# A reordered expert loop with a lag of three, and a narrow selecting matmul in the rotary attention

## The chip, the cores and the metric

The kernel runs on one core of one Trainium2 chip. The metric is device time in microseconds (us), from the start to the end of one execution. Besides TensorE (PE), VectorE (DVE), ScalarE (ACT) and GpSimd (POOL) the core has SyncE (SP), which here only issues DMAs.

## The reference, cut to what matters

Four layers, each an attention-like part and a feed-forward-like part with a layer norm before and after and a residual sum. The activations are 4096 tokens of 128 numbers. Two of the eight parts are touched.

```python
def _L2_ffn_ref(x, gate_w, ln_w, ln_b, fc1s, b1s, fc2s, b2s):   # expert choice: 8 experts, each takes its 512 best tokens
    scores = jax.nn.softmax(xf @ gate_w.T, axis=-1)
    vals, idx = jax.lax.top_k(scores.T, k)
    y = xf[flat_idx].reshape(k, n, d)
    y = (y - mu) * jax.lax.rsqrt(var + LN_EPS) * ln_w + ln_b
    h = jax.nn.gelu(jnp.einsum('knd,nfd->knf', y, fc1s) + b1s, approximate=True)
    out = (jnp.einsum('knf,ndf->knd', h, fc2s) + b2s) * kept_w[..., None]
    xf = xf.at[flat_idx].add(out.reshape(k * n, d))

def _L3_attn_ref(x, Wqkv, bqkv, Wout, bout):                    # rotary attention: 16 heads of 8 numbers
    q, k = _apply_rope(q, cos, sin), _apply_rope(k, cos, sin)
    attn = jax.nn.softmax(jnp.einsum('bhqd,bhkd->bhqk', q, k) / scale, axis=-1)
    out = jnp.einsum('bhqk,bhkd->bhqd', attn, v)
    return out.transpose(0, 2, 1, 3).reshape(b, t, d) @ Wout.T + bout
```

## The kernel before, in words

The program is a row of stages; all activations stay in on-chip memory. Within a stage every engine has its own instruction stream, written out by hand, and semaphores order them. Engines execute their streams in program order. At the end of a stage the engines meet.

**Expert choice** (`expert_choice`). After the thresholds and ranks are found, a loop goes over the 8 experts `e`. For each expert five engines' worth of steps follow one another:

- `slots(e)` on DVE (L2218 to L2229) compares slot numbers and makes the one-hot matrices of expert `e`: L2222, L2224, and four pieces at L2228. There are two buffers, `e % 2`.
- `find(e)` on PE (L2094 to L2100) multiplies them, 32 matmuls in four pieces of 8; each piece waits for its piece of L2228.
- `picks(e)` on DVE (L2231 to L2237) turns the result into token indices and weights.
- `gather(e)` on POOL (L2056 to L2060) issues four indirect DMAs that fetch the tokens' rows.
- `tokens(e)` on PE transposes them (L2107), ScalarE copies them (L2185), `up(e)` on PE (L2116) makes 4 chunks of the hidden layer, ScalarE applies the GELU (L2191), `down(e)` on PE (L2125, L2126) makes the output.
- `output(e)` on DVE (L2245) weighs it, into one of two `out` buffers.
- `scatter(e)` on POOL (L2062 to L2069) issues four indirect DMAs that add it to the result in DRAM. It waits for the DMAs of `scatter(e - 1)` to have landed. POOL's order is gather 0, 1, 2, scatter 0, gather 3, scatter 1, and so on, then scatters 6 and 7.

PE's order (L2153 to L2161, `LAG = 2`) is find 0, find 1, then in each further round `e`: tokens, up of `e - 2`, find of `e`, down of `e - 2`. DVE's order (L2292 to L2299) is slots 0, picks 0, slots 1, picks 1, slots 2, picks 2, slots 3, output 0, picks 3, slots 4, output 1, picks 4, and so on.

**Rotary attention** (`attention_layer` with `rope`, 32 rounds `i`, each for 512 tokens and 4 heads). In a round PE makes scores for the row maxima (`max_tile`, L720, into two double banks shared with `pick` in a ring, reduced by DVE at L921), scores for the exponential (L733, ScalarE at L836), and the product with the values (L743). DVE copies that product to `o_quad` (L933). It is laid out with heads along partitions: head `g` at partitions `32 g` to `32 g + 7`, its softmax denominator at `32 g + 8`. `pick(i)` (L747 to L754) brings it back to tokens along partitions: four PE transposes of 128x128 (L752). `normalise(i)` on DVE takes reciprocals (L950) and multiplies (L952), and so frees the bank of the ring for the second `max_tile` after it.

**Setup** issues the small loads of constants on SP (L103, then `RotaryTables.load` and `MixtureInputs.load`), and turns the square weights on PE and ScalarE (L117).

Of the kernel before, what the change touches and what calls it, by code (L numbers as in the profile page):

```python
# [14 lines left out]
TPB = S // 128  # L15
HEADS, HD = 16, 8
# [378 lines left out]
def attention_layer(c, tag, w, scale, tables=None, reload=None):  # L395
# [5 lines left out]
    nc = c.nc  # L401
# [45 lines left out]
    maxes = Ring([c.bank(0, 2), c.bank(2, 2)], for_vector())  # L447
# [26 lines left out]
    ordered, q_pads, k_pads, k_ones = sem("ordered"), sem("q_pads"), sem("k_pads"), sem("k_ones")  # L474
    pool_step, dve_step = sem("pool_step"), sem("dve_step")
    if rope:
        qk_bias, v_bias, cos_t, sin_t = tables.qk_bias, tables.v_bias, tables.cos, tables.sin
        w_swap = c.take(256).rearrange("p (w c) -> p w c", w=2)
        other = both()
        swapped, summed, picked = sem("swapped"), sem("summed"), sem("picked")  # L480
        fetched = [sem(f"fetched{b}") for b in range(B)]
        of_o = LayerNorm(c, f"{tag}_norm_o")
# [32 lines left out]
    with nc.Block() as block:  # L515
# [163 lines left out]
        def _(pe):  # L679
# [67 lines left out]
            def pick(i):  # L747

                pe.wait_ge(out_taken, i + 1)
                pe.wait_ge(max_taken, maxes.room(("pick", i)))  # L750
                for t in range(4):
                    last = nc.tensor.transpose(maxes.bank(("pick", i))[:, 128 * t:128 * t + 128],  # L752
                                               o_quad[:, i % 2, 128 * t:128 * t + 128], c.ident)
                last.then_inc(max_made, 1)  # L754

            pe.wait_ge(ordered, 1)
# [122 lines left out]
        def _(dve):  # L879
# [55 lines left out]
            def normalise(i):  # L935

                b, s = divmod(i, TPB)
                if by_tokens:
                    dve.wait_ge(out_taken, i + 1)
                    o = o_quad[:, i % 2, :].rearrange("p (j r) -> p j r", r=32)  # L940
                    nc.vector.reciprocal(recip[:, i % 2, :], o[:, :, HD]).then_inc(recip_done, 1)
                    dve.wait_ge(recip_done, i + 1)
                    nc.vector.tensor_tensor(c.o[:, i, :].rearrange("p (j d) -> p j d", d=HD), o[:, :, 0:HD],
                                            recip[:, i % 2, :].unsqueeze(2).to_broadcast([128, HEADS, HD]),
                                            ALU.mult).then_inc(o_done, 1)
                else:
                    dve.wait_ge(max_made, maxes.count(("pick", i)))
                    o = maxes.bank(("pick", i))[:, 0:512].rearrange("p (t g r) -> p t g r", t=TPB, g=4)
                    r = recip[:, i % 2, :].rearrange("p (t g) -> p t g", t=4)
                    nc.vector.reciprocal(r, o[:, :, :, HD]).then_inc(recip_done, 1)  # L950
                    dve.wait_ge(recip_done, i + 1)
                    nc.vector.tensor_tensor(c.o[:, TPB * b:TPB * b + TPB, 32 * s:32 * s + 32].rearrange("p t (g d) -> p t g d", g=4),  # L952
                                            o[:, :, :, 0:HD],
                                            r.unsqueeze(3).to_broadcast([128, TPB, 4, HD]), ALU.mult).then_inc(max_taken, 1)
                    dve.wait_ge(max_taken, maxes.count(("pick", i)))
                    dve.sem_inc(o_done, 1)
# [536 lines left out]
EXPERTS, FFN = 8, 512  # L1493
# [420 lines left out]
def expert_choice(c, d, n_count):  # L1914

    nc = c.nc
# [53 lines left out]
    GROUPED = 6 + ROUNDS * TRIALS  # L1970
    GROUP = TILES // 2
    EARLY = 20
    LAG = 2
    weight_bank = lambda g: c.bank(5 + g % 3)
    count_bank, iota_bank, hot_bank = c.bank(0)[:, 0:TRIALS], c.bank(1)[:, 0:128], c.bank(0)
    limit_bank = c.bank(0)[:, 64:64 + EXPERTS]
# [1 line left out]
    with nc.Block() as block:  # L1978
# [104 lines left out]
        def _(pe):  # L2083
# [10 lines left out]
            def find(e):  # L2094
                for h in range(PIECES):
                    pe.wait_ge(hot, PIECES * e + h + 1)
                    for t in range(TILES // PIECES * h, TILES // PIECES * (h + 1)):
                        last = nc.tensor.matmul(hot_bank[:, 128 + 20 * e:148 + 20 * e], one_hot[:, e % 2, t, :],
                                                vals[:, e % 2, t].rearrange("p v b -> p (v b)"), start=(t == 0), stop=(t == TILES - 1))
                last.then_inc(hot_used, 1)  # L2100

            def tokens(e):
                pe.wait_ge(got[e], 16 * PER_EXPERT)
                if e >= 1:
                    pe.wait_ge(yT_done, e)
                for s in range(PER_EXPERT):
                    last = nc.tensor.transpose(c.bank(2)[:, 128 * s:128 * s + 128], rows[:, PER_EXPERT * e + s, :], c.ident)  # L2107
                last.then_inc(y_turned, 1)

            def up(e):  # L2110
                pe.wait_ge(yT_done, e + 1)
                for k in range(CHUNKS):
                    n = CHUNKS * e + k
                    if n >= 3:
                        pe.wait_ge(h_done, n - 2)
                    nc.tensor.matmul(c.bank(3 + n % 3), fc1[:, e, k, :], yT[:, e % 2, :], start=True, stop=True).then_inc(h_made, 1)  # L2116
# [34 lines left out]
            turn_weights(6, 2 * EXPERTS - 6)  # L2151
            pe.wait_ge(w_copied, 2 * EXPERTS)
            for e in range(EXPERTS + LAG):  # L2153
                if e >= LAG:
                    tokens(e - LAG)
                    up(e - LAG)
                if e < EXPERTS:
                    pe.wait_ge(planes, 3)
                    find(e)
                if e >= LAG:  # L2160
                    down(e - LAG)  # L2161

# [32 lines left out]
        def _(dve):  # L2195
# [22 lines left out]
            def slots(e):  # L2218
                s, at = e % 2, slice(TILES * e, TILES * e + TILES)
                if e >= 2:  # L2220
                    dve.wait_ge(hot_used, e - 1)
                ch.next(tt(here[:, s], slot_tile[:, at].unsqueeze(2).to_broadcast([128, TILES, PER_EXPERT]),  # L2222
                           slots_of[:, e, :].unsqueeze(1).to_broadcast([128, TILES, PER_EXPERT]), ALU.is_equal))
                tt(vals[:, s], plane[:, e, :, 0:VALS].unsqueeze(3).to_broadcast([128, TILES, VALS, PER_EXPERT]),  # L2224
                   here[:, s].unsqueeze(2).to_broadcast([128, TILES, VALS, PER_EXPERT]), ALU.mult)
                n = TILES // PIECES
                for h in range(PIECES):
                    tt(one_hot[:, s, n * h:n * h + n, :], lane[:, TILES * e + n * h:TILES * e + n * h + n].unsqueeze(2).to_broadcast([128, n, 128]),  # L2228
                       iota_bank.unsqueeze(1).to_broadcast([128, n, 128]), ALU.is_equal).then_inc(hot, 1)  # L2229
# [9 lines left out]
            def output(e):  # L2239
                dve.wait_ge(o_made, e + 1)  # L2240
                if e >= 2:
                    dve.wait_ge(added, 16 * PER_EXPERT * (e - 1))
                for s in range(PER_EXPERT):
                    n = PER_EXPERT * e + s
                    ts(out[:, e % 2, s, :], c.bank(6 + e % 2)[:, 128 * s:128 * s + 128], weight[:, n:n + 1], None, ALU.mult).then_inc(o_done, 1)  # L2245
# [43 lines left out]
            ch.mark(ts(slot_tile, whole, 7, None, ALU.logical_shift_right))  # L2289
            ch.next(ts(lane, whole, 127, None, ALU.bitwise_and))  # L2290
            dve.wait_ge(planes, 3)
            slots(0)  # L2292
            for e in range(EXPERTS + LAG):
                if e < EXPERTS:
                    picks(e)
                if e + 1 < EXPERTS:
                    slots(e + 1)
                if e >= LAG:
                    output(e - LAG)  # L2299
    return result.rearrange("(t p) c -> p t c", p=128)  # L2300


# [342 lines left out]
def shape_constants():  # L2645

    import numpy as np
    half = HD // 2
    freq = (1.0 / np.float32(10000.0) ** (np.arange(0, HD, 2, dtype=np.float32) / np.float32(HD))).astype(np.float32)
    angle = np.outer(np.arange(S, dtype=np.float32), freq)  # L2650
    row = np.arange(128)
    width = row // 4 % HD
    sign = np.where(width < half, -1.0, 1.0).astype(np.float32)
    number = (np.arange(4)[None, :] - row[:, None]) % 4 + 1
    return {"rope_cos": np.cos(angle).astype(np.float32).T[width % half].copy(),
            "rope_sin": (np.sin(angle).astype(np.float32).T[width % half] * sign[:, None]).astype(np.float32),
            "expert_below": np.where(number == 1, -1.0, number - 1.0).astype(np.float32),
            "expert_share": (1.0 / number).astype(np.float32)}

# [10 lines left out]
class RotaryTables:  # L2670


    def __init__(self, c):
        self.qk_bias = c.take(4)
        self.v_bias = c.take(D)
        self.cos, self.sin = c.take(S), c.take(S)
        self.loads = 4

    def load(self, eng, d, signal):
        eng.dma_start(self.qk_bias, d["qk_bias"]).then_inc(signal, 16)  # L2680
        eng.dma_start(self.v_bias, d["L3_attn_bqkv"][2 * D:3 * D].partition_broadcast(128)).then_inc(signal, 16)
        eng.dma_start(self.cos, d["rope_cos"]).then_inc(signal, 16)
        eng.dma_start(self.sin, d["rope_sin"]).then_inc(signal, 16)


def rotary_attention(c, d, tables, reload):
# [57 lines left out]
```

## Time and profile before

| | |
|---|---|
| median of 3 runs | 2099.89 us (2098.89 to 2099.98) |
| profiled execution: its own time | 2098.89 us |
| profiled execution: its span | 2097.2 us |
| around the span | 1.7 us |
| TensorE busy over the span | 1577.8 us (75%) |
| VectorE, ScalarE, GpSimd busy | 1231.0, 1100.2, 781.0 us (59%, 52%, 37%) |
| mean granted TensorE clock | 0.824 of 2.4 GHz |

The shares are averages over stages that have different limits, so they say little about one stage. The loop over experts lies between 1187 and 1310 us of the span, the rotary attention's rounds between about 1400 and 1824 us.

### The profile page before, as it was taken

The numbers are of one execution on the slowest core, as the hardware profiler recorded it, in microseconds if no ns is written. First come the engines' busy times: TensorE is split into PE (matmuls) and PEld (weight loads), VectorE is DVE, ScalarE is ACT, GpSimd is POOL, SyncE is SP. The second block draws the span as 40 slices with busy tenths as digits, with TensorE's granted clock in tenths as the row PEclk, the third lists the DMA queues.
The fourth block names the chain that finished last, engine by engine and source line by source line (L and its number), as shares of the span: only waits on it lengthen the run. The fifth ranks groups of instructions, "written<-read, shape, count | busy, mean of one in ns | idle before, by whom it ended". The sixth has DMA issues, their size and how long they took to land. (4 is left out here: it accounts for less than half of the span.)

```text
span 2097.2 us, 25624 instructions
## 1 busy us (share of the span) xinstructions
PE 1577.8 (75%) x8295; PEld 807.5 (39%) x8295; DVE 1231.0 (59%) x2804; ACT 1100.2 (52%) x2209; POOL 781.0 (37%) x1456
## 2 busy tenths in 40 slices
PE   2799999992658882433544397379999999879998
PEld 1133333321445561332433265113333333457776
DVE  3688888866633322025457852668888878435543
ACT  2277777774234331115654432237777777645553
POOL 3444555416253334245016277514444430012211
PEclk8699999995755555675765599569999999989999
DMA  3211211100000003110001423211111111010000
GB/s 98 78 62 65 66 65 62 65 10 0 2 0 1 1 0 115 32 28 4 0 1 49 123 38 36 64 64 60 58 58 60 62 61 48 3 41 11 11 6 16
DMA packets 84969, 85.16 MB, mean 41 GB/s; under 512 B 35942, under 2 KB 67536, under 8 KB 84708
## 3 DMA queue, kind: packets, MB, share of 16 engines
q1 hardware_dynamic: 74340, 76.35, 11.1%
q0 software_dynamic: 7680, 6.06, 1.8%
q10 hardware_dynamic: 2816, 1.12, 0.2%
q8 instruction: 67, 1.10, 0.2%
q14 instruction: 66, 0.54, 0.1%
HBM read 59.76 MB, written 25.17 MB: 40 GB/s over the span
## 5 line engine op out<-in xcount | busy, mean ns | idle before, releaser
L921 DVE TENSOR_REDUCE arena<-psum 128x2 f32<-128x1024 f32 x512 | 601.9, 1217 | 130.3 <-PE psum L720 126.0
L836 ACT ACTIVATE arena<-psum 128x512 f32<-128x512 f32 x1024 | 553.6, 595 | 141.4 <-PE psum L733 132.4
L733 PE MATMUL psum<-arena 99*128 99x512 bf16 x1024 | 313.2, 387 | 16.1 <-DMA arena<-arena 11.5
L720 PE MATMUL psum<-arena 72*128 72x512 bf16 x1024 | 287.6, 397 | 40.7 <-POOL arena L622 18.4
L743 PE MATMUL psum<-arena 128*32 128x512 f32 x2048 | 274.5, 608 | 3.1 <-ACT arena L836 1.9
L733 PEld LDWEIGHTS psum<-arena 99*128 99x128 bf16 x1024 | 74.8, 98 | 294.4 <-ACT arena L836 223.7
L720 PEld LDWEIGHTS psum<-arena 72*128 72x128 bf16 x1024 | 95.9, 99 | 184.4 <-DVE arena L921 28.5
L2419 ACT ACTIVATE arena<-arena 128x128 f32<-128x128 f32 x252 | 102.5, 481 | 94.7 <-POOL arena L2407 94.7
L2402 POOL TENSOR_SCALAR arena<-arena 128x4 f32<-128x4 f32 x80 | 22.4, 281 | 304.9 <-DVE arena L2396 300.1
L631 POOL TENSOR_TENSOR arena<-arena 128x16 bf16<-128x16 f32 x64 | 13.8, 216 | 307.1 <-DVE arena L921 215.3
L344 ACT ACTIVATE arena<-arena 128x128 f32<-128x128 f32 x192 | 76.7, 480 | 96.3 <-POOL arena L260 70.9
L2532 ACT ACTIVATE arena<-psum,arena 128x512 f32<-128x512 f32 x128 | 84.3, 682 | 77.5 <-PE psum L2484 75.5
L622 POOL COPY arena<-arena 72x1024 f32<-72x1024 f32 x64 | 64.9, 1042 | 153.2 <-PE psum L733 129.1
L2496 PEld LDWEIGHTS psum<-arena 128*128 128x128 f32 x1024 | 118.1, 192 | 8.2 <-issue 8.2
L2496 PE MATMUL psum<-arena 128*128 128x128 f32 x1024 | 119.9, 275 | 0.0
L2484 PE MATMUL psum<-arena 128*128 128x512 f32 x256 | 117.0, 601 | 0.0
L332 PE MATMUL psum<-arena 128*128 128x128 f32 x96 | 26.7, 434 | 116.6 <-ACT arena L344 116.6
L2617 DVE SCALAR_TENSOR_TENSOR arena<-psum,arena 128x128 f32<-128x128 f32 x128 | 36.0, 344 | 127.2 <-PE psum L2496 126.5
L2393 DVE BATCH_NORM_STATS2 arena<-arena 128x6 f32<-128x128 f32 x320 | 69.0, 278 | 63.0 <-PEq L100 21.4
L2405 POOL TENSOR_TENSOR arena<-arena 128x4 f32<-128x4 f32 x80 | 83.1, 1039 | 6.7
L743 PEld LDWEIGHTS psum<-arena 128*32 128x32 f32 x2048 | 40.4, 108 | 109.5 <-ACT arena L836 60.9
L332 PEld LDWEIGHTS psum<-arena 128*128 128x128 f32 x96 | 17.7, 223 | 123.4 <-ACT arena L344 123.4
(425 smaller groups left out, 2562.6 us busy)
## 6 DMA issues: line engine op xcount, KB each, us to landing
arena<-L_q_parts SPq DMA_DIRECT2D x192, 96.0 KB
arena<-L_k_parts SPq DMA_DIRECT2D x192, 96.0 KB
L_q_parts<-arena SPq DMA_DIRECT2D x16, 384.0 KB, 3.3
L_k_parts<-arena SPq DMA_DIRECT2D x16, 384.0 KB, 3.2
arena<-in_L_ffn_w SPq DMA_DIRECT2D x1, 2048.0 KB, 10.7
ec_result<-arena SPq DMA_DIRECT2D x1, 2048.0 KB, 9.8
arena<-in_L_ffn_fc2s SPq DMA_DIRECT2D x1, 2048.0 KB, 17.5
ec_normed<-arena SPq DMA_DIRECT2D x2, 1024.0 KB, 7.6
```

The lines of the kernel that those rows point to most:

```text
L344: nc.scalar.activation(dst[:, t, :], src[:, t, :], ACT.Identity, bias=f.shift[:, t:t + 1], scale=f.scale[:, t:t + 1]).then_inc(signal, 1)
L720: last = nc.tensor.matmul(bank[:, 512 * h:512 * h + 512], columns(q9[0:QK_ROWS], i, m // 2, 128 * (2 * (m % 2) + h), 128), columns(k9[0:QK ...
L733: nc.tensor.matmul(acts.bank(name), columns(k9[0:ROWS], i, g, 128 * k, 128), columns(q9[0:ROWS], i, g, 0, 512), start=True, stop=True).the ...
L743: last = nc.tensor.matmul(out_bank[32 * g:32 * g + 32, :], v32[:, i % 2, g, k, :], prob[:, k % 2, g, :], start=(k == 0), stop=(k == 3))
L836: nc.scalar.activation(prob[:, k % 2, g, :], acts.bank(name), ACT.Exp, scale=scale).then_inc(act_taken, 1)
L921: nc.vector.tensor_reduce(neg_max[:, i % 2, 2 * m:2 * m + 2], maxes.bank(("max", i, m)).rearrange("p (h t) -> p h t", h=2), axis=AX.X, op= ...
L2393: self.nc.vector.bn_stats(self.stats[:, t, :], src[:, t, :]).then_inc(self.stats_done, 1)
L2405: self.nc.gpsimd.tensor_tensor(self.scale[:, at], self.var_eps[:, at], self.minus_half[:, 0:TPB], ALU.pow).then_inc(self.scale_done, 1)
L2419: self.nc.scalar.activation(dst[:, t, :], src[:, t, :], ACT.Identity, bias=self.shift[:, t:t + 1], scale=self.scale[:, t:t + 1]).then_inc( ...
L2484: nc.tensor.matmul(c.bank(k), w1[:, e, 128 * k:128 * k + 128], c.nT[:, b, 1:S + 1], start=True, stop=True).then_inc(h_made, 1)
L2496: last = nc.tensor.matmul(c.bank(4 + g % 2)[:, 128 * t:128 * t + 128], hT[:, g % 2, k, 128 * t:128 * t + 128], w2[:, e, k, :], start=(k == ...
L2532: nc.scalar.activation(hT[:, g % 2, k, :], c.bank(k), ACT.Relu, bias=b1T[:, CHUNKS * e + k:CHUNKS * e + k + 1]).then_inc(h_done, 1)
```

## The change

Three edits.

1. In the rotary attention the four transposes of `pick(i)` become four FP32 matmuls of the same `o_quad` blocks (as weights) with a constant 128x36 matrix `select`. It selects the 32 useful rows and the 4 denominators, so a bank holds 4 x 36 columns in place of 4 x 128. The DVE instructions read the new layout.
2. The constant is one more load (128x36 FP32) on SP in setup, and 36 words of on-chip memory.
3. In `expert_choice` `LAG` becomes 3. PE's round `e` is now find of `e`, tokens and up of `e - 2`, down of `e - 3`. DVE's loop is written as slots, output of `e - LAG`, picks.

```diff
-                    last = nc.tensor.transpose(maxes.bank(("pick", i))[:, 128 * t:128 * t + 128],
-                                               o_quad[:, i % 2, 128 * t:128 * t + 128], c.ident)
+                    last = nc.tensor.matmul(maxes.bank(("pick", i))[:, 36 * t:36 * t + 36], o_quad[:, i % 2, 128 * t:128 * t + 128],
+                                            select, start=True, stop=True)
...
-                    o = maxes.bank(("pick", i))[:, 0:512].rearrange("p (t g r) -> p t g r", t=TPB, g=4)
+                    o = maxes.bank(("pick", i))[:, 0:144].rearrange("p (t r) -> p t r", r=36)
-                    nc.vector.reciprocal(r, o[:, :, :, HD]).then_inc(recip_done, 1)
+                    nc.vector.reciprocal(r, o[:, :, 32:36]).then_inc(recip_done, 1)
...
-    LAG = 2
+    LAG = 3
...
             for e in range(EXPERTS + LAG):
-                if e >= LAG:
-                    tokens(e - LAG)
-                    up(e - LAG)
                 if e < EXPERTS:
                     pe.wait_ge(planes, 3)
                     find(e)
+                if 2 <= e < EXPERTS + 2:
+                    tokens(e - 2)
+                    up(e - 2)
                 if e >= LAG:
                     down(e - LAG)
...
-            slots(0)
             for e in range(EXPERTS + LAG):
                 if e < EXPERTS:
-                    picks(e)
-                if e + 1 < EXPERTS:
-                    slots(e + 1)
+                    slots(e)
                 if e >= LAG:
                     output(e - LAG)
+                if e < EXPERTS:
+                    picks(e)
...
+    select = np.zeros((128, 36), np.float32)
+    for g in range(4):
+        for r in range(HD):
+            select[32 * g + r, HD * g + r] = 1.0
+        select[32 * g + HD, 4 * HD + g] = 1.0
...
+        eng.dma_start(self.select, d["select_rows"]).then_inc(signal, 16)
```

## Rows read from the trace of the kernel before

**Rows 1.** The page's first line.

```profile
span 2097.2 us, 25624 instructions
```

**Rows 2.** Timeline of POOL, expert loop: start, length in us, engine, line, operation, count, [idle before].

```profile
1199.12 1.00 POOL L2059 DMA_INDIRECT arena<-ec_normed,arena  x1 [0.30 <-issue]
...
1218.18 1.63 POOL L2068 DMA_INDIRECT ec_result<-arena  x1 [1.68 <-DVE arena L2245]
...
1231.06 1.62 POOL L2068 DMA_INDIRECT ec_result<-arena  x1 [0.30 <-issue]
...
1238.56 1.09 POOL L2059 DMA_INDIRECT arena<-ec_normed,arena  x1 [0.30 <-issue]
...
1242.60 0.99 POOL L2059 DMA_INDIRECT arena<-ec_normed,arena  x1 [0.30 <-issue]
1243.90 1.62 POOL L2068 DMA_INDIRECT ec_result<-arena  x1 [0.30 <-issue]
...
1292.53 1.55 POOL L2068 DMA_INDIRECT ec_result<-arena  x1 [2.62 <-DMA ec_result<-arena]
...
1302.21 1.55 POOL L2068 DMA_INDIRECT ec_result<-arena  x1 [2.56 <-DMA ec_result<-arena]
```

**Rows 3.** Timeline of DVE in the same loop.

```profile
1201.93 4.61 DVE L2228 TENSOR_TENSOR arena<-arena,psum 128x1024 bf16<-128x1024 int32 x4
...
1216.17 1.12 DVE L2245 TENSOR_SCALAR arena<-psum,arena 128x128 f32<-128x128 f32 x4
...
1257.94 0.18 DVE L2234 COPY arena<-psum 128x20 f32<-128x20 f32 x1 [4.62 <-PE psum L2098]
...
1259.70 4.61 DVE L2228 TENSOR_TENSOR arena<-arena,psum 128x1024 bf16<-128x1024 int32 x4
```

**Rows 4.** Timeline of PE in the same loop.

```profile
1199.75 0.39 PE L2098 MATMUL psum<-arena 128*128 128x20 bf16 x8 [0.74 <-DVE arena L2228]
1201.71 1.11 PE L2107 MATMUL psum<-arena 128*128 128x128 f32 x4 [1.57 <-DMA arena<-ec_normed,arena]
...
1208.90 0.95 PE L2098 MATMUL psum<-arena 128*128 128x20 bf16 x32
...
1251.89 0.66 PE L2107 MATMUL psum<-arena 128*128 128x128 f32 x4
...
1256.95 0.95 PE L2098 MATMUL psum<-arena 128*128 128x20 bf16 x32
1257.89 1.16 PE L2125 MATMUL psum<-arena 128*128 128x128 f32 x8
...
1263.49 0.48 PE L2126 MATMUL psum<-arena 1*128 1x128 f32 x2
```

**Rows 5.** Windows, PE alone: stretch, its length, busy us (instructions), granted clock, DMA share, GB/s.

```profile
1190.00:1194.00 4.00, 1.45 (x34) 0.93 0.02 4
1202.00:1207.00 5.00, 4.13 (x8) 0.50 0.15 39
1301.00:1309.00 8.00, 0.00 (x0) 0.60 0.29 26
1410.00:1814.00 404.00, 394.64 (x2181) 1.00 0.15 54
```

**Rows 6.** Timeline of all engines around one `pick` of the rotary attention.

```profile
1562.42 0.60 PE L752 MATMUL psum<-arena 128*128 128x128 f32 x4
...
1563.06 0.26 DVE L950 RECIPROCAL arena<-psum 128x16 f32<-128x16 f32 x1 [0.49 <-PE psum L752]
...
1563.69 0.61 PE L720 MATMUL psum<-arena 72*128 72x512 bf16 x2 [0.24 <-DVE arena L952]
```

**Rows 7.** Timeline of PE in the last stage: four one-column FP32 matmuls.

```profile
1882.12 0.95 PE L2472 MATMUL psum<-arena 128*128 128x1 f32 x8
```

**Rows 8.** Timeline of setup: SP's last load, ScalarE's last copy.

```profile
12.20 0.43 SPq L2374 DMA_DIRECT2D arena<-in_L_ffn_b  x1
...
20.35 0.60 ACT L117 ACTIVATE arena<-psum 128x512 f32<-128x512 f32 x1 [0.26 <-PE psum L140]
```

**Rows 9.** DMA view: issues of a kind, count, size and median us to landing.

```profile
arena<-in_L_ffn_b SPq DMA_DIRECT2D x1, 8.0 KB, 5.6
```

More of the change, by code:

```diff
@@ L476, in attention_layer @@
     if rope:
-        qk_bias, v_bias, cos_t, sin_t = tables.qk_bias, tables.v_bias, tables.cos, tables.sin
+        qk_bias, v_bias, cos_t, sin_t, select = tables.qk_bias, tables.v_bias, tables.cos, tables.sin, tables.select
         w_swap = c.take(256).rearrange("p (w c) -> p w c", w=2)
@@ L947, in normalise @@
                     dve.wait_ge(max_made, maxes.count(("pick", i)))
-                    o = maxes.bank(("pick", i))[:, 0:512].rearrange("p (t g r) -> p t g r", t=TPB, g=4)
+                    o = maxes.bank(("pick", i))[:, 0:144].rearrange("p (t r) -> p t r", r=36)
                     r = recip[:, i % 2, :].rearrange("p (t g) -> p t g", t=4)
-                    nc.vector.reciprocal(r, o[:, :, :, HD]).then_inc(recip_done, 1)
+                    nc.vector.reciprocal(r, o[:, :, 32:36]).then_inc(recip_done, 1)
                     dve.wait_ge(recip_done, i + 1)
                     nc.vector.tensor_tensor(c.o[:, TPB * b:TPB * b + TPB, 32 * s:32 * s + 32].rearrange("p t (g d) -> p t g d", g=4),
-                                            o[:, :, :, 0:HD],
+                                            o[:, :, 0:32].rearrange("p t (g d) -> p t g d", g=4),
                                             r.unsqueeze(3).to_broadcast([128, TPB, 4, HD]), ALU.mult).then_inc(max_taken, 1)
@@ L2656, in shape_constants @@
             "rope_sin": (np.sin(angle).astype(np.float32).T[width % half] * sign[:, None]).astype(np.float32),
+            "select_rows": select,
             "expert_below": np.where(number == 1, -1.0, number - 1.0).astype(np.float32),
@@ L2676, in __init__ @@
         self.cos, self.sin = c.take(S), c.take(S)
-        self.loads = 4
+        self.select = c.take(36)
+        self.loads = 5
     def load(self, eng, d, signal):
```

## The prediction

> **What bounds the kernel now.** I read the page's first line for the span [rows 1], then the two touched stages in the timeline, one engine at a time, because an average over 2097 us hides what sets the pace of a loop.
>
> In the expert loop the reader is to look at POOL first [rows 2]. A scatter group starts at 1231.06, a gather group at 1238.56, the next scatter group at 1243.90. So four scatters take 7.50 us, four gathers 5.34 us, and a POOL round takes 12.84 us with only 0.30 us of issue between instructions: POOL sets the pace from its first scatter (1218.18) on. PE's round is nearly as long: from `down` at 1257.89 to the end of its last matmul, 1263.49 + 0.48 = 1263.97, is 6.08 us, and from `tokens` at 1251.89 to `find` at 1256.95 is 5.06 us [rows 4]. With `find` (0.94 us) that is 12.0 us, and PE is never idle long. DVE is idle half the time, but where its work lies matters: the timeline shows picks at 1257.94 and slots until 1259.70 + 4.61 = 1264.31 [rows 3], which is exactly while PE does `down` [rows 4]. The 6.4 us of DVE work that the next `find` needs are hidden behind the 6.1 us of `down`.
>
> In the rotary attention PE is busy 394.6 of 404 us at full clock [rows 5], so what lengthens PE's stream there lengthens the kernel. After a `pick` PE also waits for DVE: it starts at 1562.42, its matmuls end at 1563.02, the reciprocal starts at 1563.06, and only at 1563.69, after 0.24 us idle, does PE get the bank back [rows 6]. The chain pick, reciprocal, multiply, `max_tile` is on the path.
>
> **The change, part by part.**
>
> *DVE in the expert loop.* Writing both loops out gives the same order: slots 3, output 0, picks 3, slots 4, output 1, picks 4. Nothing of DVE's stream moves. Only PE's does, and with it the moment at which each `output` can run.
>
> *PE in the expert loop.* `find(e + 1)` now comes first in its round, right behind `down(e - 3)`. DVE's order between those two is output of `e - 3`, picks of `e`, slots of `e + 1`. The output waits for that same `down`; queued behind it on DVE are the picks and the slots, and for the slots waits `find(e + 1)`, behind which on PE `tokens`, `up` and the next `down` stand. The loop is closed: PE waits through all of the DVE work, and DVE then waits through all of PE's. What `down` used to hide is now bare. The terms of a round:
>
> - signal from PE to DVE: 0.04 us, as from 1563.02 to 1563.06 [rows 6];
> - output: 1.12 us [rows 3];
> - picks and slots: 1257.94 to 1264.31 = 6.37 us [rows 3];
> - last piece of `find` after the last piece of slots: 0.39 us [rows 4]; the other three pieces run under the slots.
>
> That is 7.92 us in which PE has next to nothing to do. Then `tokens` and `up`, 5.06 us, and `down`, 6.08 us. A round at full clock takes 19.06 us, far over POOL's 12.84, so POOL no longer sets the pace.
>
> The clock adds to that. In the stretch 1190 to 1194, where PE is busy 1.45 of 4 us with pieces of `find`, the granted clock goes from full to half (mean 0.93); it is still 0.50 from 1202 to 1207, while `tokens(0)` and `up(0)` run; and behind the last `down` it falls within the stretch from 1301 to 1309, in which PE does nothing (mean 0.60, so full for about its first 1.6 us) [rows 5]. A gap of 7.9 us with only pieces of `find` in it is like the first of these, so I take it that each round starts at half clock. At half clock `tokens(0)` to the end of `up(0)` took 1201.71 to 1208.90 = 7.19 us instead of 5.06 [rows 4], so 2.13 us more. A round is then 21.19 us. The Trainium skill, "TensorE: Matmul & The Clock Gate", section "The HAM clock gate", has the rule that an idle TensorE is gated to half rate and sustained work releases it, and its section "HAM oscillation" warns of loops that go cold in each pass, which speaks against this change. By that rule the round is the 21.19 us of the rows, and without it 19.06 us, the first rival below.
>
> *The rounds added up.* Slots 2 ends at 1201.93 + 4.61 = 1206.54 [rows 3]; `find(2)` at 1206.93; the third picks come earlier than before, since `find(2)` used to start at 1208.90 [rows 4]. Then `tokens(0)` and `up(0)` at half clock, to 1214.12; slots 3 are there by 1213.3, so `find(3)` takes 0.95, to 1215.07; `tokens(1)` and `up(1)`, to 1220.13; `down(0)`, to 1226.2. Rounds 4 to 7 close the loop: 4 x 21.19 = 84.8, so `down(4)` ends at E = 1311.0.
>
> The drain follows from E. `tokens(6)`, `up(6)`, `down(5)` need no slots: E + 11.14. Output 4 lets scatter 4 start at E + 2.05 (from output's start to the scatter's is 1216.17 to 1218.18, 2.01 us [rows 2, 3]). Scatter 4 takes 7.50; gather 7 is queued behind it on POOL; its last DMA starts 4.04 later (1238.56 to 1242.60) and lands 2.59 us after that (1199.12 to 1201.71) [rows 2, 4]. So `tokens(7)` starts at E + 16.18, 5.0 us late and at half clock: `up(7)` ends at E + 23.37, `down(6)` at E + 29.45. Scatter 6 starts at E + 31.5 and scatter 7, which waits for scatter 6 to land, 1302.21 - 1292.53 = 9.68 us later [rows 2]: E + 41.18 = 1352.1. Before it was 1302.21. The expert stage gets 49.9 us longer. The stages behind it start from its end and are not changed by that.
>
> *The pick.* A transposition is one PE record: four, 0.60 us [rows 6]. An FP32 matmul is two records: four matmuls with 128x128 weights and a single moving column are 8 records in 0.95 us [rows 7]. So the price lies in the loads and not in the columns, and 36 columns are near to one. The end of `pick` moves by 0.95 - 0.60 = 0.35 us, and with it reciprocal, multiply and the bank. DVE's two instructions keep their element counts. Over 32 rounds: 11.2 us. Bounds: the bf16 matmuls of `find` with 20 columns run at 0.95 / 32 = 0.03 us each [rows 4]; 8 such records would take 0.24 us where the transposes take about 0.44, which is -0.2 x 32 = -6.5 us. From above, weight loads at 1.16 us for 8 records [rows 4] give 0.56 more than 0.60, 18 us; I take 0.35, since rows 7 has the same type, weights and number of records.
>
> The Trainium skill is split here. "TensorE: Matmul & The Clock Gate", section "Terms", says that the transpose mode is four times faster for FP32; counting columns alone, 4 x 36 against 128, the pick would cost +0.03 us a round, 0.9 us in all. Its section "LDWEIGHTS" says that a load takes as long as its weights have columns, 107 ns for 128; eight in place of four would be +0.43 us a round, an estimate of 13.7 us. The second is what rows 7 looks like.
>
> *The load in setup.* SP's last load is issued at 12.20 and 5.6 us go by to landing [rows 8, 9]: 17.8, one more issue of about 0.5 makes it 18.3. ScalarE's last copy ends at 20.95 [rows 8], which hides it. Without that cover it would cost 0.5 us. I take 0.
>
> Sum: 2098.89 (the profiled execution's own time) + 49.9 + 11.2 = 2160.0 us. The median of the runs shown lies 1.0 us over that execution; I leave this inside the range.
>
> **The rivals.**
>
> - *The clock stays up, or comes back at once.* For it: `find` pieces run in the gap. Against: such pieces did not keep it up at 1194 [rows 5]. The four rounds are 19.06 us (E = 1302.4) and the last `up` 2.13 us shorter: expert stage +39.3, time 2149. 15%.
> - *The clock comes back later.* `tokens` and `up` wholly at half clock would lose up to twice the 2.13 us. Six such starts: up to 13 us more, 2172. 12%.
> - *The pick costs nothing.* The records overlap with their neighbours. 2149. 8%.
> - *POOL stays the bound.* If something breaks the loop (`find` served by slots made before the output), a PE round is under 12.84 us, all is hidden and the earlier picks give back up to 2.9 us of POOL's start: 2098.9 - 2.9 + 11.2 = 2107. Against it stands the written order on DVE. 3%.
> - *The other side: the narrow pick is cheap and decides.* At the lower bound, -6.5 us, the kernel would get faster, to 2092, but only if the expert loop is hidden behind POOL too, that is, its PE round is under 12.84 us. The pick's price changes sign where a record takes under 0.44 / 8 = 0.055 us; rows 7 shows about 0.1. 2%.
>
> **How the numbers follow.** The forecast has 60%: each wait follows from the program's order, and the prices are rows of the same shapes. The range takes in the clock and pick rivals up to their times and the pick's bounds: 2147 to 2172. About 0.2% (4 us) is what a measurement of this kernel can tell from no change. All cases but the last end slower by more than that: slower 0.96; I leave 0.02 for no change, where the terms would have to cancel, and 0.02 for faster.
>
> **What would show it.** In the changed kernel's trace `find`'s idle time before it should be on DVE L2228, some 4 us whole and then in three pieces, in rounds 4 to 7; the DVE output should start about every 21 us rather than every 12; the POOL should idle 8 us a round before each scatter group; the granted clock should fall to 0.5 in each round. Slots and picks should keep their durations. In the attention the 4 transposes become 8 records of about 0.1 us, and PE's wait for the multiply should stay, with rounds 0.35 us longer. The prediction is wrong if DVE reaches slots before an output, if PE's round is below 13 us, or if the selecting matmuls are one record each.

## The result, and the profile after

The changed kernel takes 2165.14 us (median of 4 runs, 2164.86 to 2165.86); beside it the kernel before took 2099.93. The ratio is 1.031, 95% interval 1.029 to 1.032: it is slower by 65 us. The forecast was 2160.0 with a range of 2147 to 2172. The profiled execution of the changed kernel took 2162.47 us, 63.6 more than that of the kernel before, where the forecast's sum was 61.1 more.

The timeline of VectorE (DVE) in the changed kernel's expert loop, to be held against [rows 3]:

```profile
1248.28 1.13 DVE L2245 TENSOR_SCALAR arena<-psum,arena 128x128 f32<-128x128 f32 x4 [14.12 <-PE psum L2126]
1249.32 0.17 DVE L2234 COPY arena<-psum 128x20 f32<-128x20 f32 x1
...
1251.06 4.61 DVE L2228 TENSOR_TENSOR arena<-arena,psum 128x1024 bf16<-128x1024 int32 x4
...
1269.28 1.13 DVE L2245 TENSOR_SCALAR arena<-psum,arena 128x128 f32<-128x128 f32 x4 [13.61 <-PE psum L2126]
```

DVE waits 14 us for the end of `down`, and then does output, picks and slots in a row, to 1255.67. Picks and slots take as long as before. TensorE (PE) in the same round, against [rows 4]:

```profile
1247.75 0.48 PE L2126 MATMUL psum<-arena 1*128 1x128 f32 x2
1252.42 0.36 PE L2098 MATMUL psum<-arena 128*128 128x20 bf16 x8 [4.19 <-DVE arena L2228]
...
1255.73 0.39 PE L2098 MATMUL psum<-arena 128*128 128x20 bf16 x8 [0.75 <-DVE arena L2228]
1255.96 1.09 PE L2107 MATMUL psum<-arena 128*128 128x128 f32 x4
1257.92 5.51 PE L2116 MATMUL psum<-arena 128*128 128x512 f32 x8 [0.87 <-ACT arena L2185]
1263.27 1.05 PE L2125 MATMUL psum<-arena 128*128 128x128 f32 x8
...
1326.76 1.11 PE L2107 MATMUL psum<-arena 128*128 128x128 f32 x4 [5.20 <-DMA arena<-ec_normed,arena]
```

The idle time before `find` has moved to DVE L2228: 4.19 us whole, then between the pieces. From 1247.75 + 0.48 = 1248.23 to `tokens` at 1255.96 PE has 7.7 us with four short pieces in it. `tokens` (1.09 for 0.66) and `up` (5.51 for 3.70) then run longer. The last row is the wait of `tokens(7)` for its gather. The windows of PE in the round before (columns as in [rows 5]) show why they are longer:

```profile
1226.00:1230.00 4.00, 0.72 (x5) 1.00 0.00 0
1230.00:1236.00 6.00, 2.47 (x36) 0.57 0.37 33
1236.00:1240.00 4.00, 3.60 (x5) 0.50 0.31 49
1240.00:1243.00 3.00, 3.00 (x12) 0.81 0.20 49
```

The clock is full at the gap's start, at half from within it, and full again towards the end of `up`. POOL, against [rows 2], is idle 15 us ahead of the first scatter group and 8 to 9 us ahead of the next four, and no longer sets the pace:

```profile
1228.77 1.63 POOL L2068 DMA_INDIRECT ec_result<-arena  x1 [14.97 <-DVE arena L2245]
...
1250.21 1.61 POOL L2068 DMA_INDIRECT ec_result<-arena  x1 [8.87 <-DVE arena L2245]
...
1352.05 1.55 POOL L2068 DMA_INDIRECT ec_result<-arena  x1 [2.51 <-DMA ec_result<-arena]
```

The last scatter group starts at 1352.05, before at 1302.21 [rows 2]. In the rotary attention a PE row of one pick, against [rows 6]:

```profile
1617.63 0.98 PE L752 MATMUL psum<-arena 128*128 128x36 f32 x8
1618.44 0.60 PE L720 MATMUL psum<-arena 72*128 72x512 bf16 x2
1619.29 0.60 PE L720 MATMUL psum<-arena 72*128 72x512 bf16 x2 [0.25 <-DVE arena L952]
```

Four matmuls are 8 records (a record is one instruction as the profile lists it), 0.98 us where the transpositions took 0.60, and the wait for the multiply behind them is what it was. What follows on PE starts 0.81 us after the first record; in the kernel before it started 0.43 us after 1562.42 [rows 6]:

```profile
1562.85 0.60 PE L720 MATMUL psum<-arena 72*128 72x512 bf16 x2
```

### The profile page after: what moved, and what is told of

Its sections match the earlier page's. It is cut to its first block and busy times, and to the rows that moved or that the text cites. A ratio compares the mean times of both kernels' runs of the same rounds, so it can differ in the third digit from the quotient of the medians.

```text
span 2160.8 us, 25881 instructions
## 1 busy us (share of the span) xinstructions
PE 1600.1 (74%) x8423; PEld 826.0 (38%) x8423; DVE 1232.1 (57%) x2804; ACT 1100.4 (51%) x2209; POOL 781.3 (36%) x1456
## 5 line engine op out<-in xcount | busy, mean ns | idle before, releaser
L631 POOL TENSOR_TENSOR arena<-arena 128x16 bf16<-128x16 f32 x64 | 13.8, 216 | 318.3 <-DVE arena L921 223.9
L2495 PEld LDWEIGHTS psum<-arena 128*128 128x128 f32 x1024 | 118.1, 192 | 8.2 <-issue 8.2
L2392 DVE BATCH_NORM_STATS2 arena<-arena 128x6 f32<-128x128 f32 x320 | 69.0, 278 | 66.3 <-DMA arena<-ec_result 21.9
L2068 POOL DMA_INDIRECT ec_result<-arena x32 | 50.3, 1572 | 68.3 <-DVE arena L2245 58.2
```

The source lines that it names most:

```text
L2392: self.nc.vector.bn_stats(self.stats[:, t, :], src[:, t, :]).then_inc(self.stats_done, 1)
L2495: last = nc.tensor.matmul(c.bank(4 + g % 2)[:, 128 * t:128 * t + 128], hT[:, g % 2, k, 128 * t:128 * t + 128], w2[:, e, k, :], start=(k == ...
```

## The experiments

Twelve more kernels ran. Time beside that of the kernel before on the same chip; "loop" is measured in the profiled execution from the start of `find(0)` to the start of the last scatter group, and is 111.2 us before (1190.98 to 1302.21) and 160.9 changed.

| kernel | us | before | ratio, 95% interval | loop us |
|---|---|---|---|---|
| loops only | 2152.8 | 2100.1 | 1.025, 1.023 to 1.027 | 161.0 |
| pick only | 2113.8 | 2100.1 | 1.006, 1.0045 to 1.008 | 111.3 |
| open loop | 2139.7 | 2100.1 | 1.019, 1.017 to 1.020 | 136.6 |
| filled gap | 2151.4 | 2100.1 | 1.024, 1.023 to 1.026 | 149.2 |
| wide matmul | 2114.5 | 2100.6 | 1.006, 1.005 to 1.008 | 111.1 |
| find behind up | 2139.7 | 2100.6 | 1.019, 1.017 to 1.020 | 137.0 |
| constant only | 2100.5 | 2100.6 | 1.000, 0.999 to 1.001 | 111.1 |
| gather ahead | 2124.6 | 2100.6 | 1.012, 1.010 to 1.013 | 119.7 |
| find behind up, filled | 2141.5 | 2100.3 | 1.019, 1.018 to 1.021 | 136.4 |
| before, filled | 2100.6 | 2100.3 | 1.000, 0.999 to 1.001 | 109.7 |
| lag of three, repaired | 2103.3 | 2100.3 | 1.002, 1.001 to 1.003 | 114.9 |
| find first | 2111.6 | 2101.1 | 1.005, 1.0035 to 1.007 | 120.9 |

**The two parts apart.** *Loops only*, on the changed kernel:

```diff
-                    last = nc.tensor.matmul(maxes.bank(("pick", i))[:, 36 * t:36 * t + 36], o_quad[:, i % 2, 128 * t:128 * t + 128],
-                                            select, start=True, stop=True)
+                    last = nc.tensor.transpose(maxes.bank(("pick", i))[:, 128 * t:128 * t + 128],
+                                               o_quad[:, i % 2, 128 * t:128 * t + 128], c.ident)
```

> The changed kernel with the pick put back to four transpositions; the expert loop keeps the lag of three and both new orders. If the two parts add up and the closed loop is the large one: 2165.1 less the 11.4 us by which the 32 picks stretched in the changed kernel's trace = 2153.7 us, PE rounds of the expert loop still 20.6 to 21.5 us. If the pick is hidden or the two parts interact (the pick only costs because of the later start): 2165 us.

*Pick only* is the kernel before with that edit the other way round, the constant and its load.

> The kernel before with the selecting matmul, its constant and its load alone; expert loop as before. If a pick's price is the 8 records: 2099.9 + 11.4 = 2111.3 us, rounds of the attention 0.37 us longer. If the price goes by moving columns (36 against 128): 2100.8 us. If the pick is hidden: 2099.9 us.

Measured: 2152.8 and 2113.8 us. The loops alone cost 52.7 us, the pick alone 13.7 us by the runs; together 66.3, and the whole change 65.2. The parts add up. In the traces the 31 rounds from the first to the last reciprocal (L950) take 410.6 us with transpositions and 421.9 with the selecting matmul, 11.3 us, as in the changed kernel (422.0). The 2 us beyond that lie inside the interval of the runs (9.5 to 16.4 us).

**Is it the slots behind the output?** *Open loop*, on the changed kernel, DVE alone:

```diff
+            slots(0)
             for e in range(EXPERTS + LAG):
                 if e < EXPERTS:
-                    slots(e)
+                    picks(e)
+                if e + 1 < EXPERTS:
+                    slots(e + 1)
                 if e >= LAG:
                     output(e - LAG)
-                if e < EXPERTS:
-                    picks(e)
```

> The changed kernel with VectorE's loop in another order: picks of e, slots of e + 1, and only then the output of e - 3. PE's order and the lag stay. If the time is lost because the slots stand behind an output that waits for down: PE no longer waits for slots, its round is 12.0 us, POOL with 12.84 us sets the pace again, and only the later first scatter is left (1228.8 in the changed kernel, 1218.2 before, 10.6 us): 2099.9 + 10.6 + 11.4 = 2121.9 us. If it is find's place in front of tokens, or the lag as such, that costs the 50 us: 2165 us, unchanged.

Measured: 2139.7 us. The wait for slots is gone and half of the expert loop's loss with it (25.4 us longer than before instead of 49.7), so the closed loop is shown. But I had expected 2121.9. PE's timeline in this run has another wait:

```profile
1239.21 0.97 PE L2098 MATMUL psum<-arena 128*128 128x20 bf16 x32
1243.88 1.12 PE L2107 MATMUL psum<-arena 128*128 128x128 f32 x4 [3.71 <-DMA arena<-ec_normed,arena]
1245.86 5.10 PE L2116 MATMUL psum<-arena 128*128 128x512 f32 x8 [0.87 <-ACT arena L2185]
```

`tokens(3)` waits 3.7 us for its gather, `tokens(5)` 3.6, `tokens(7)` 5.3, and each then finds the clock at half. `gather(3)` stands on POOL behind `scatter(0)`, which waits for `output(0)`. With a lag of three that comes one round later, while `tokens(3)` stays in its round: output, scatter, gather and landing take 16.3 us in this run (1227.55 to 1243.88), a PE round 11.8.

*Gather ahead* takes the open loop and moves the gather:

```diff
             for e in range(EXPERTS):
                 gather(e)
-                if e == 2:
+                if e == 3:
                     pool.wait_ge(xf_out, 16)
-                if e >= 2:
-                    scatter(e - 2)
-            scatter(EXPERTS - 2)
-            scatter(EXPERTS - 1)
+                if e >= 3:
+                    scatter(e - 3)
+            for e in range(EXPERTS - 3, EXPERTS):
+                scatter(e)
```

> The kernel with the open loop (picks, slots of e + 1, output of e - 3 on VectorE), and on POOL gather(e) now stands ahead of scatter(e - 3), not behind it. In the open-loop run tokens of experts 3, 5 and 7 waited 3.7, 3.6 and 5.3 us for their gathers. If these gathers were late only because they stood on POOL behind a scatter that the lag had made late: those waits vanish, rounds of PE 11.8 us, POOL paces with 12.8 us from scatter 0 and the last scatter starts near 1310: 2120 us. If the waits have another cause (the DMAs themselves): 2139 us.

Measured: 2124.6 us, loop 119.7 (before + 8.5, where a last scatter near 1310 means about 8). The waits of `tokens` are gone, and POOL issues back to back from its first scatter, 1232.22, to scatter 5 at 1293.66. Scatter 6 then waits 3.72 us for its output, so at the end PE's rounds count again. Two of them took 13.5 us instead of 11.8, partly at half clock (last section). So the lag has a price of its own, through POOL's order.

**Is it the clock?** *Filled gap* adds matmuls that the result doesn't use to the changed kernel:

```diff
+            def warm(n):
+                for _ in range(n):
+                    nc.tensor.matmul(c.bank(3)[:, 0:384], c.ident, c.wT[:, 0:3, :].rearrange("p w c -> p (w c)"), start=True, stop=True)
...
+                    if e >= 4 and h >= 1:
+                        pe.wait_ge(h_done, CHUNKS * (e - 2))
+                        warm(1)
                     pe.wait_ge(hot, PIECES * e + h + 1)
...
                 if e >= LAG:
                     down(e - LAG)
+                    if e < EXPERTS - 1 or e == EXPERTS:
+                        pe.wait_ge(h_done, CHUNKS * (e - 1))
+                    if e < EXPERTS - 1:
+                        warm(6)
+                    elif e == EXPERTS:
+                        warm(8)
```

> The changed kernel with matmuls of no use to the result added in PE's gaps: six of 384 columns behind each of down(0) to down(3), one between the pieces of find(4) to find(7), eight before tokens(7). Each is estimated at 0.65 us. If the clock's fall in the gaps costs what the rows at both levels differ by: tokens and up take 5.1 us instead of 7.0 to 8.0, five times, 10 us in all, granted clock 1.00 through the loop, 2155 us. If the clock is not what lengthens them, or does not stay up by it: 2165 us or, if the added matmuls delay find, up to 2175 us.

Measured: 2151.4 us, 13.8 less than the changed kernel, the loop 11.7 less. Added work made the kernel faster. PE's windows and timeline of this run:

```profile
1228.00:1325.00 97.00, 91.12 (x495) 1.00 0.24 30
```

```profile
1236.04 0.64 PE L2114 MATMUL psum<-arena 128*128 128x128 f32 x4
1237.55 3.70 PE L2123 MATMUL psum<-arena 128*128 128x512 f32 x8 [0.87 <-ACT arena L2198]
1241.09 1.05 PE L2132 MATMUL psum<-arena 128*128 128x128 f32 x8
...
1254.76 0.64 PE L2114 MATMUL psum<-arena 128*128 128x128 f32 x4
```

The clock is full throughout, `up` takes 3.70 us again, and a round 1254.76 - 1236.04 = 18.72 us. What is left is the closed loop without the fall of the clock.

**Where on PE does find have to stand?** *Find behind up*, on the changed kernel, PE alone:

```diff
             for e in range(EXPERTS + LAG):
+                if 2 <= e < EXPERTS + 2:
+                    tokens(e - 2)
+                    up(e - 2)
                 if e < EXPERTS:
                     pe.wait_ge(planes, 3)
                     find(e)
-                if 2 <= e < EXPERTS + 2:
-                    tokens(e - 2)
-                    up(e - 2)
```

> The changed kernel, with find of e back behind tokens and up of e - 2 on PE; lag of three and VectorE's order as in the changed kernel. VectorE's output, picks and slots (7.9 us with the last piece of find) then run beside tokens and up (5.1 us), not in a bare gap. If it is find's place together with the slots behind the output that closes the loop: PE rounds of 14.0 us, clock mostly full, and the last expert still late by its gather: 2127 us, with 3 either way. If slots behind the output costs the same wherever find stands: 2165 us.

Measured: 2139.7 us. Find's place together with DVE's order closes the loop; but the time is again 13 us more than expected. In this run's timeline one `down` runs at half clock (2.08 us where 1.16 are usual), and later `tokens(4)` and `tokens(5)` wait 1.2 and 1.4 us for their gathers:

```profile
1235.02 2.08 PE L2125 MATMUL psum<-arena 128*128 128x128 f32 x8
...
1256.67 0.66 PE L2107 MATMUL psum<-arena 128*128 128x128 f32 x4 [1.24 <-DMA arena<-ec_normed,arena]
```

I first took the falls of the clock for the whole reason. *Find behind up, filled* fills the gaps between the last pieces of find (one matmul of 384 columns ahead of each of the last two pieces, e from 3 on):

> The run with find behind up (2139.7 us, 12.7 more than I had expected), with one matmul of 384 columns and no use to the result ahead of each of the last two pieces of find, for experts 3 to 7. In that run the granted clock fell at 1230.8, beside the late pieces of find, and stayed at half until 1247.3, through all of down. If these falls of the clock are the whole of the miss: clock 1.00, PE rounds of 14.0 us, 2129 us. If they are a by-product of waits: no change, 2140 us.

Measured: 2141.5 us, so that theory fell. The filled run's own timeline shows what took the clock's place:

```profile
1240.67 0.66 PE L2113 MATMUL psum<-arena 128*128 128x128 f32 x4 [2.41 <-DMA arena<-ec_normed,arena]
...
1255.69 0.66 PE L2113 MATMUL psum<-arena 128*128 128x128 f32 x4
...
1271.89 0.66 PE L2113 MATMUL psum<-arena 128*128 128x128 f32 x4 [2.37 <-DMA arena<-ec_normed,arena]
```

The clock now stays full through that `down`, but `tokens(3)` and `tokens(5)` wait for their gathers, and the `up` behind them runs partly at half clock (5.40 and 5.32 us). Counted from `find(0)`, `tokens(3)` starts only 1.4 us earlier than without the filling (48.1 us, 49.6 without). So in the run without filling the slow `down` hid the late gather, and taking away the fall of the clock alone gains almost nothing. I had reckoned with a gather's wait for `tokens(7)` only. That late gathers and the clock behind them make up the miss is argued from this trace and from the pair *open loop* and *gather ahead*; find behind up with its gathers ahead and nothing else changed wasn't run.

*Find first* puts find ahead of tokens in the kernel before, lag of two, other engines as before:

```diff
             for e in range(EXPERTS + LAG):
+                if e < EXPERTS:
+                    pe.wait_ge(planes, 3)
+                    find(e)
                 if e >= LAG:
                     tokens(e - LAG)
                     up(e - LAG)
-                if e < EXPERTS:
-                    pe.wait_ge(planes, 3)
-                    find(e)
-                if e >= LAG:
                     down(e - LAG)
```

> The kernel before, and on PE only find of e moved ahead of tokens and up of e - 2; lag of two, VectorE's and POOL's orders as before, so the loop is open. tokens(0) waits for find(2), so down(0) and the first scatter come 4 us later than before. If find's place has no other price: 2104.3 us, clock at 1.00 from the first up on. In the run with gathers ahead the clock fell twice, for about 4 us each, with PE hardly idle, where find's 20-column matmuls, the transpositions and the wait for ScalarE stand next to each other; if that is a price of find's place, it is here too: PE rounds with a fall take 1.7 us more, 2104 to 2109 us.

Measured: 2111.6 us, above both. The clock stayed up. PE rounds are 12.81 us (`find` starts at 1225.06, 1237.87, 1250.68): find used to cover the last GELU between `up` and `down`, and with it moved `down` waits 0.8 us for ScalarE. The first scatter comes 5.7 us later, counted from `find(0)`, and the last 9.6: the last two scatter groups wait 3.65 and 4.90 us for their outputs, so PE's longer rounds set the time there. So find's place in front costs about 10 us even with the lag of two and an open loop.

**What is the pick's price?** *Wide matmul*, on the kernel before:

```diff
-                    last = nc.tensor.transpose(maxes.bank(("pick", i))[:, 128 * t:128 * t + 128],
-                                               o_quad[:, i % 2, 128 * t:128 * t + 128], c.ident)
+                    last = nc.tensor.matmul(maxes.bank(("pick", i))[:, 128 * t:128 * t + 128], o_quad[:, i % 2, 128 * t:128 * t + 128],
+                                            c.ident, start=True, stop=True)
```

> The kernel before; only the four transpositions of a pick become four FP32 matmuls with the same 128x128 identity, so 128 moving columns in place of the 36 of the selecting matmul, and the bank's layout stays. If a record's price is its weight load: 8 records at 1.16/8 = 0.11 to 0.145 us, the pick's end 0.45 to 0.56 us later than with transpositions, 14 to 18 us, 2114 to 2118 us, hardly more than the selecting matmul's. If the moving columns set the price, 3.6 times the selecting matmul's 0.37 us a round: 43 us, 2143 us.

Measured: 2114.5 us, 13.9 us more than before, where 36 columns cost 13.7. In the traces the difference is a little larger: the 31 rounds take 424.3 us, 13.7 more than with transpositions, against 11.3 for 36 columns. With 128 columns the pick costs nearly what it costs with 36:

```profile
1569.03 1.05 PE L752 MATMUL psum<-arena 128*128 128x128 f32 x8
1569.92 0.60 PE L720 MATMUL psum<-arena 72*128 72x512 bf16 x2
1570.76 0.61 PE L720 MATMUL psum<-arena 72*128 72x512 bf16 x2 [0.24 <-DVE arena L952]
```

*Constant only* is the kernel before with the constant, its load and the 36 words, which nothing reads.

> The kernel before with the constant, its load in setup and the 36 words alone, which nothing reads. Asks where the 2 us go that the selecting matmul alone cost beyond its 32 rounds. If the load and the shifted memory cost nothing: 2099.5 to 2101 us. If they slow something in the stages ahead of the expert loop: 2102 us.

Measured: 2100.5 us against 2100.6. Load and memory cost nothing.

**A version that beats both?** *Before, filled* has the `warm` matmuls ahead of `tokens(0)`, in the kernel before:

> The kernel before with matmuls of no use to the result (384 columns) in PE's gaps ahead of tokens(0): one ahead of each of the last three pieces of find(0) and find(1), four behind find(0), two behind find(1). In the kernel before PE does tokens(0) and up(0) at half clock, 7.2 us in place of 5.1, and the first scatter at 1218.2 paces all that follows. If that is so: first scatter and end 2.1 us earlier, 2098.4 us, at the edge of what can be measured; the trace decides. If the added matmuls delay the finds or the first scatter waits for something else: 2100.5 us or more.

Measured: 2100.6 against 2100.3 us. `tokens(0)` to `up(0)` took 5.06 us at full clock and the loop became 1.5 us shorter in the trace, but the runs can't tell it from no change.

*Lag of three, repaired* has transpositions, find behind up, slots ahead of the output and the gathers ahead, all edits shown above:

> A lag of three with everything that was found to cost put right: transpositions in the pick, find behind up on PE, slots of e + 1 ahead of the output on VectorE, gather(e) ahead of scatter(e - 3) on POOL. down(0) ends near 1222.7 (before 1215.9), so the first scatter starts 6.6 us later than before, one gather less stands behind it (5.3 us), one more landing is waited for bare (2.2 us): the last scatter 3.5 us later than before, 2104 us, and the clock at 1.00 from 1210 on. If the lag itself costs more than that, 2110 us or more; if it gains, under 2100 us.

Measured: 2103.3 us against 2100.3; loop 114.9, 3.6 us longer than before where 3.5 was expected. PE's window in this run:

```profile
1210.00:1290.00 80.00, 73.16 (x528) 1.00 0.26 38
```

With every wait mended a lag of three is no gain, since POOL sets the pace either way. No version ran faster than the kernel before.

## Why the prediction was right, step by step

- **DVE's order is unchanged, and the loop closes.** Right. DVE's rows come in the order written out, and *open loop* and *find behind up* each take away one side of the closure and with it about half of the expert loop's loss (25.4 and 25.8 us left of 49.7).
- **The bare stretch, 7.92 us.** Measured 7.7 us (1248.23 to 1255.96); `tokens` can start before the last piece of find has ended.
- **The clock, 2.13 us a round.** Right in kind and size on the whole. `tokens` to the end of `up` took 1255.96 to 1263.27 = 7.31 us in that round; the rounds, between the ends of `down`, were 21.5, 21.0, 20.7 and 20.6 us, forecast 21.19 each, since the clock came back at another point of `up` each time. *Filled gap* shows what it costs: 11.7 us of the loop, forecast (first rival) 10.6.
- **The drain.** E was forecast at 1311.0 and was 1310.59. `tokens(7)` started at E + 16.17 (forecast 16.18). The last scatter group started at 1352.05, forecast 1352.1. That it is hit to 0.1 us is partly luck: `down(0)` ended 0.5 us later than forecast, the four rounds took 0.9 less and the stretch from E to the last scatter 0.3 more.
- **The pick, 0.35 us a round, 11.2 us.** 0.37 us a round, 11.4 us over 31 rounds. Up to 128 columns its price lies in the number of records, as argued from [rows 7]: *wide matmul*. Counting columns, the other reading, fails: 3.6 times the columns cost under 0.1 us more. An estimate from `up` in *filled gap*: its records of 512 columns follow each other at (1241.09 - 1237.55) / 8 = 0.44 us, so columns alone would take 0.11 us a record at 128 and 0.03 at 36. Measured are 0.89 / 8 = 0.11 in *wide matmul* and 0.81 / 8 = 0.10 in the changed kernel, so at 36 columns something else than the columns sets the price. That this is the weight load fits but isn't shown by itself. The Trainium skill, "TensorE: Matmul & The Clock Gate", section "LDWEIGHTS", gives a load time by the number of weight columns, which for 128 is an estimate of 107 ns; the spacing of 0.10 to 0.11 us is near to that.
- **The load in setup costs nothing.** Right: *constant only*.
- **Taking the sum from one execution.** The 5.1 us between forecast and median are 2.4 in stretches beside the loop and the attention's rounds (1.6 between last scatter and first pick, 0.8 behind the last pick), 0.1 of the two terms, and 2.7 the distance of the profiled execution from the median: 2162.47 against 2165.14. The stages ahead of the loop, which no kernel here changed but for the load in setup, moved `find(0)` between 1190.9 and 1194.5 us from one execution to another.
- **The range's lower end.** It was said to take in the pick's bounds, but the lower one, -6.5 us, gives 2098.9 + 49.9 - 6.5 = 2142 us, under 2147. The measured pick lay far from that bound, so nothing hung on it.
- **A rival that was thought too simple.** I wrote that if the loop were broken POOL would set the pace again and only the pick be left, 2107 us. *Open loop* broke it and took 2139.7. The gather behind a later scatter, on POOL, was a second closure that I had seen only for expert 7. It was hidden in the changed kernel because the first was longer: rounds of 21 us against the 16.2 us of that chain.

## What to carry to other kernels

Before lengthening a software pipeline, write out each engine's stream and look for pairs of waits that point at each other across one round: a step taken later must not have something queued behind it that an earlier step needs, on any engine and on the DMA-issuing one too. A closed loop costs the sum of both engines' work, and mending it uncovers the next one, so each mend needs its own run. A narrower matmul saves little where the number of records sets the pace (36 columns instead of 128: under 0.1 us of 0.9), and a transposition (one record) replaced by an FP32 matmul (two) cost nearly double here (0.43 us became 0.81 for four).

## What the runs showed of the hardware that I had not expected

The clock can fall while PE is hardly idle. In *gather ahead* PE was busy in all but 0.9 us between the start of `find(5)`, 1241.87, and the half clock:

```profile
1241.87 0.97 PE L2098 MATMUL psum<-arena 128*128 128x20 bf16 x32
1242.69 0.64 PE L2107 MATMUL psum<-arena 128*128 128x128 f32 x4
1244.19 5.40 PE L2116 MATMUL psum<-arena 128*128 128x512 f32 x8 [0.87 <-ACT arena L2185]
```

```profile
1244.00:1248.00 4.00, 3.81 (x5) 0.58 0.30 47
```

The same steps in *find first* (1237.87 to 1241) kept 1.00. And in *find behind up* PE was busy throughout a stretch at half clock, doing the 128-column matmuls of `down` one behind another:

```profile
1230.00:1240.00 10.00, 10.00 (x47) 0.53 0.25 41
```

The clock came back only during the 512-column matmuls of the next `up`. How busy PE looks in the profile doesn't explain these two rows. The Trainium skill, "TensorE: Matmul & The Clock Gate", section "The HAM clock gate", has the rule that an idle TensorE is lowered to half rate and sustained work releases it: the changed kernel's rows agree with it, and by itself it doesn't explain these two. Why the same steps lowered it in one run and not in another stays open.
